# Routed steps: the key kept in a register, the opening step fed from buffered records, counters at the step's end, the result added by VectorE

## The reference

```python
def step(h, p):
    op = jnp.argmax(h[0, 0, :NOPS])
    q = h @ p['wq'][op]; k = h @ p['wk'][op]; v = h @ p['wv'][op]
    attn = softmax(einsum('bqd,bkd->bqk', q, k) * scale)
    y = einsum('bqk,bkd->bqd', attn, v) @ p['wo'][op]
    h = where(p['am'][op], y, h)
    z = relu(h @ p['w1'][op] + p['b1'][op]) @ p['w2'][op] + p['b2'][op]
    h = where(p['fm'][op], z, h)
    return h
```

## Time and profile before

| | |
|---|---|
| median of 3 runs | 333.0 us |
| profiled execution | 331.74 us |
| its span on the core | 330.0 us |
| mean granted clock of PE | 0.982 |
| busy: PE, DVE, ACT, POOL | 294.5, 189.0, 154.4, 35.1 us |
| start of the first key's `MAX8` | 246.66 us |

### The profile page before, as it was taken

How to read it: one execution, slowest core, us unless ns; L and a number is a source line. 1 busy time by engine, 2 the same in 40 slices (tenths; PEclk the granted TensorE clock), 3 DMA queues, 4 the chain that set the end, 5 groups by cost and what they waited for, 6 DMA issues and landing times.

```text
span 330.0 us, 6721 instructions
## 1 busy us (share of the span) xinstructions
PE 294.5 (89%) x2064; PEld 199.4 (60%) x2064; DVE 189.0 (57%) x452; ACT 154.4 (47%) x336; POOL 35.1 (11%) x34
## 2 busy tenths in 40 slices
PE   7999999999999989999999989989996779777980
PEld 3665677777444437898999645668952266226620
DVE  4594998883346676478887564462261156225720
ACT  2097766667154256445566033112203448644840
POOL 5300062000100014000220000024200000000010
PEclk9999999999999999999999999999998799999997
DMA  2954300000000000000000033333100100000000
GB/s 84 248 113 89 88 9 2 2 0 2 2 0 0 0 1 2 0 2 0 3 0 0 0 58 62 68 68 63 31 2 3 21 2 0 19 19 0 0 18 32
DMA packets 9386, 9.17 MB, mean 28 GB/s; under 512 B 4080, under 2 KB 8944, under 8 KB 9072
## 3 DMA queue, kind: packets, MB, share of 16 engines
q1 hardware_dynamic: 9096, 8.53, 11.7%
q10 hardware_dynamic: 264, 0.30, 0.3%
HBM read 8.57 MB, written 0.26 MB: 27 GB/s over the span
## 4 chain that ended last, share of the span: by engine, by line
PE 32%; DVE 10%; issue 4%; ACT 2%; DMA 2%; DVEq 2%; SPq 0%; POOL 0%; ACTq 0%; POOLq 0%
PE ps L759 3%; PE ps L765 3%; DMA recA<-rec_a 2%; PE ps L915 2%; PE ps L999 2%; PE ps L1055 2%; PE ps L1002 2%; PE ps L528 2%; PE ps L1047 2%; PE ps L905 1%; PE ps L897 1%; PE ps L1012 1%; PE ps L776 1%; PE ps L806 1%; DVE arena L1562 1%
## 5 line engine op out<-in xcount | busy, mean ns | idle before, releaser
L528 PE MATMUL ps<-xC,cstb 128*128 128x512 f32 (+3 forms) x134 | 57.3, 554 | 0.0
L1407 DVE TENSOR_TENSOR arena<-arena 128x512 f32 x72 | 44.3, 684 | 7.8 <-ACT arena L1107 4.6
L1114 ACT ACTIVATE arena<-ps 128x512 f32<-128x512 f32 x72 | 37.7, 603 | 15.7 <-PE ps L585 15.6
L528 PEld LDWEIGHTS ps<-xC,cstb 128*128 128x128 f32 x134 | 23.7, 192 | 24.1 <-issue 23.9
L585 PE MATMUL ps<-cstb,arena 128*128 128x128 f32 x288 | 36.3, 277 | 0.7 <-DVE arena L1407 0.7
L585 PEld LDWEIGHTS ps<-cstb,arena 128*128 128x128 f32 x288 | 31.0, 140 | 9.4 <-DVE arena L1407 8.6
L593 PE MATMUL ps<-arena 128*32 128x256 f32 x288 | 19.2, 385 | 0.0
L1275 ACT ACTIVATE arena<-ps,rmax 128x256 f32<-128x256 f32 x32 | 14.7, 479 | 2.6 <-DVE rmax L1738 2.4
L759 PE MATMUL ps<-arena 128*128 128x160 f32 x96 | 14.5, 304 | 0.3 <-DVE arena L1590 0.3
L1055 PE MATMUL ps<-arena,w2c 128*32 128x512 f32 x32 | 12.0, 719 | 1.9 <-ACT arena L1306 1.9
L497 POOL TENSOR_TENSOR arena<-w32b,cstb 128x1024 f32<-128x1024 f32 x4 | 7.6, 1893 | 57.5 <-PEq L891 45.8
(11 more groups left out here) (373 smaller groups left out, 529.0 us busy)
## 6 DMA issues: line engine op xcount, KB each, us to landing
arena<-rec_a SPq DMA_DIRECT2D x19, 128.5 KB
toepb<-toep SPq DMA_DIRECT2D x1, 1536.0 KB
w32b<-w SPq DMA_DIRECT2D x1, 1225.0 KB
cstb<-cst SPq DMA_DIRECT2D x1, 1044.0 KB
recA<-rec_a SPq DMA_DIRECT2D x4, 128.5 KB
arena<-rec_b SPq DMA_DIRECT2D x19, 16.5 KB
w1b<-moe_w SPq DMA_DIRECT2D x1, 264.0 KB
xC<-x SPq DMA_DIRECT2D x1, 256.0 KB, 2.6
```

The source lines that it names most:

```text
L528: mm(ps[bank][:, 0:cols], ident if lhs is None else lhs, (xC if rhs is None else rhs)[:, 0:cols], start=True, stop=True)
L1114: af(SQ[:, c].rearrange("p q n -> p (q n)"), ps[c % BI], ACT.Copy).then_inc(S["s_ev"], 1)
L1407: tt_(ST[:, c], hy.unsqueeze(3).to_broadcast([P, PT, 16, 16]), hx.unsqueeze(2).to_broadcast([P, PT, 16, 16]), ALU.mult).then_inc(S["prod"], 1)
```

## The change

The key's register lives through the loops: `following` loads it once at a step's end, after `op_ev`, and a turn of a loop only copies and compares it. The check of the key's bounds is gone. The counters of a step without attention are raised at its end instead of in an `Else` branch. For the opening step PE reads the key ahead of the transposes of `T` and ACT ahead of the copy of `tC`; the transposes go to PSUM bank 3, and of the three pairs of clock-keeping matmuls around them one stays. DVE copies `w2c` straight from `cacheB` and `b2c` from `recA` before the step. ACT brings in one table, with an `Exp` of 1x1, ahead of `hC`'s first copy; the 1x1 Relu is gone. The column of the table is copied to `tab_col` ahead of the attention. DVE writes `outC` from the PSUM bank in every step, just ahead of `hC`; POOL adds only where no step runs, and no longer takes part in the steps, so `op_read` counts three engines from then on. DVE waits for `op_read` ahead of `f1t`. SP stores before it waits for the last record. The 1x1 tile `f1_first` becomes `exp_first`; `tab_col` is a new tile of 1x19.

```diff
-            return eng.value_load(a, min_val=CODE0, max_val=CODE0 + NOPS * PER_OP - 1)
+            return eng.value_load(a)
...
+
+        def following(eng, key):
+
+            eng.reg_load(key, keyi[0:1, 0:1])
+            eng.reg_alu(key, key, PER_OP, ALU.mod)
...
-        def routed(eng, body, k=None):
+        def routed(eng, body, k):
+            key = eng.alloc_register("next_key")
 
             def places(levels, first):
                 with eng.Fori(0, levels[0]) as i:
-                    k = chosen(eng)
+                    k = eng.snap(key)
                     with eng.If(k >= ACTIVE):
                         n = eng.snap(first + i)
                         if len(levels) == 1:
-                            body(eng.snap(n + 1), k)
+                            body(eng.snap(n + 1), k, key)
                         else:
                             places(levels[1:], n * levels[1])
 
-            k = chosen(eng) if k is None else k
             with eng.If(k >= ACTIVE):
-                body(0, k)
+                body(0, k, key)
                 places(PLACES, 0)
...
-                sp.wait_ge(S["out_ready"], 1)
...
-                v = code_at(sp, keyi[0:1, 0:1])
+                following(sp, key)
+                v = sp.snap(key)
                 rec = record_of(sp, v)
                 sp.dma_start(recA, rec_a[bass.ds(rec, 1), :, :].to_broadcast([BI, C, REC_A])
                              ).then_inc(S["w_in"], 16)
                 sp.dma_start(recB, rec_b[bass.ds(rec, 1), :, :].rearrange("a c n -> (a c) n")
                              ).then_inc(S["wb_in"], 16)
-                with sp.If(sp.snap(v % PER_OP) < ACTIVE):
+                with sp.If(v < ACTIVE):
+                    sp.wait_ge(S["out_ready"], n + 1)
+                    settled(sp)
+                    store()
                     sp.wait_ge(S["w_in"], (n + 3) * 16)
                     settled(sp)
                     sp.wait_ge(S["wb_in"], (n + 3) * 16)
                     settled(sp)
-                    store()
...
-            def add_if_last(h_count):
-                k = chosen(pool)
-                with pool.If(k < ACTIVE):
-                    pool.wait_ge(S["h_new"], h_count)
-                    settled(pool)
-                    nc.gpsimd.tensor_tensor(outC, tC, hC, ALU.add).then_inc(S["out_ready"], 1)
-
-            def step(n, k):
-                pool.sem_inc(S["op_read"], 1)
-                pool.wait_ge(S["op_ev"], n + 2)
-                settled(pool)
-                add_if_last(n + 2)
-
             pool.wait_ge(S["ct_ev"], 4)
             pool.wait_ge(S["op_ev"], 1)
-            add_if_last(1)
-            routed(pool, step)
+            k0 = chosen(pool)
+            pool.sem_inc(S["op_read"], 1)
+            with pool.If(k0 < ACTIVE):
+                pool.wait_ge(S["h_new"], 1)
+                settled(pool)
+                nc.gpsimd.tensor_tensor(outC, tC, hC, ALU.add).then_inc(S["out_ready"], 1)
...
-            keep_busy(2)
+            pe.wait_ge(S["op_ev"], 1)
+            k0 = chosen(pe)
+            keep_busy(1)
             pe.wait_ge(S["t_sum"], 6)
-            to_C(T, 0, S["ct_mm"])
-            keep_busy(1)
-            pe.wait_ge(S["ct_ev"], 4)
-            pe.wait_ge(S["op_ev"], 1)
-
-            def step(n, k):
+            to_C(T, 3, S["ct_mm"])
+
+            def step(n, k, key):
...
+                    pe.wait_ge(S["ct_ev"], 4)
...
-                with pe.Else():
-                    pe.sem_inc(S["rq_mm"], 3)
-                    pe.sem_inc(S["rv_mm"], 1)
-                    pe.sem_inc(S["sc_mm"], B)
-                    pe.sem_inc(S["pT_mm"], B)
-                    pe.sem_inc(S["ro_mm"], BG)
-                    pe.sem_inc(S["rr_mm"], 1)
+                    pe.wait_ge(S["rt_h"], n + 1)
+                    settled(pe)
...
-                    pe.wait_ge(S["rt_h"], n + 1)
...
+                with pe.If(fl < 2):
+                    pe.sem_inc(S["rq_mm"], 3)
...
                 pe.wait_ge(S["op_ev"], n + 2)
                 settled(pe)
-
-            routed(pe, step)
+                following(pe, key)
...
+            own.link(af(exp_first, ident[0:1, 0:1], ACT.Exp))
...
-            evac_C(0, tC, 5)
-
-
+            act.wait_ge(S["op_ev"], 1)
+            k0 = chosen(act)
+            evac_C(3, tC, 5)
...
-                    own.link(af(f1_first, ident[0:1, 0:1], ACT.Relu))
-                    own.restart()
-                    act.wait_ge(S["w1_bd"], n + 1)
+                    act.wait_ge(S["w1_bd"], 2 * n + 2)
...
-            def next_op(row, place):
+            def next_op(row, col):
                 link(v_.max(top8, row))
-                link(stt(cand, row, top8[0:1, 0:1], tabf[:, :, place].rearrange("p o r -> p (o r)"),
-                         ALU.is_ge, ALU.mult))
+                link(stt(cand, row, top8[0:1, 0:1], col, ALU.is_ge, ALU.mult))
                 own.restart()
                 v_.tensor_reduce(keyi.bitcast(F32), cand, AX.X, ALU.max).then_inc(S["op_ev"], 1)
 
             dve.wait_ge(S["tab_in"], 16)
-            next_op(ln_b[0:1, 0:NOPS], slice(NB, NB + 1))
+            next_op(ln_b[0:1, 0:NOPS], tabf[:, :, NB:NB + 1].rearrange("p o r -> p (o r)"))
             dve.wait_ge(S["op_ev"], 1)
             v0 = code_at(dve, keyi[0:1, 0:1])
             first_op = slot_of(dve, v0)
             dve.wait_ge(S["cache_in"], 2 * NOPS * 16)
-            link(v_.tensor_copy(recA, cacheA.rearrange("p (o n) -> p o n", o=NOPS)[:, bass.ds(first_op, 1), :]
-                                .rearrange("p o n -> p (o n)")))
-            dve.sem_inc(S["w_in"], 16)
-            link(v_.tensor_copy(recB, cacheB.rearrange("p (o n) -> p o n", o=NOPS)[:, bass.ds(first_op, 1), :]
-                                .rearrange("p o n -> p (o n)")))
-            dve.sem_inc(S["wb_in"], 16)
-            own.restart()
-
-            def step(n, k):
+            first_a = cacheA.rearrange("p (o n) -> p o n", o=NOPS)[:, bass.ds(first_op, 1), :].rearrange(
+                "p o n -> p (o n)")
+            first_b = cacheB.rearrange("p (o n) -> p o n", o=NOPS)[:, bass.ds(first_op, 1), :].rearrange(
+                "p o n -> p (o n)")
+            v_.tensor_copy(recA, first_a).then_inc(S["w_in"], 16)
+            v_.tensor_copy(w2c, first_b).then_inc(S["w1_bd"], 1)
+            dve.wait_ge(S["w_in"], 32)
+            v_.tensor_copy(b2c, recA[:, REC_A - 1:REC_A]).then_inc(S["w1_bd"], 1)
+
+            def step(n, k, key):
+                first = isinstance(n, int)
                 fl = dve.snap(k % 4)
                 ffn = dve.snap(k % 2)
-                place = place_of(dve, k)
-                with dve.If(fl < 2):
-                    dve.sem_inc(S["w_bd"], 2)
-                    dve.sem_inc(S["rq_ev"], 1)
-                    dve.sem_inc(S["sc_max"], B)
-                    dve.sem_inc(S["sc_inv"], BG)
-                    dve.sem_inc(S["pT_evD"], B - len(TURNED_ACT))
-                    dve.sem_inc(S["rt_h"], 1)
-                dve.wait_ge(S["h_new"], n + 1)
-                dve.wait_ge(S["w_in"], (n + 2) * 16)
-                settled(dve)
+                if not first:
+                    dve.wait_ge(S["h_new"], n + 1)
+                    dve.wait_ge(S["w_in"], (n + 2) * 16)
+                    settled(dve)
...
-                v_.tensor_copy(b2c, recA[:, REC_A - 1:REC_A])
-                dve.wait_ge(S["wb_in"], (n + 2) * 16)
-                v_.tensor_copy(w2c, recB).then_inc(S["w1_bd"], 1)
-                dve.wait_ge(S["w1_bd"], n + 1)
+                if not first:
+                    v_.tensor_copy(b2c, recA[:, REC_A - 1:REC_A]).then_inc(S["w1_bd"], 1)
+                    dve.wait_ge(S["wb_in"], (n + 2) * 16)
+                    v_.tensor_copy(w2c, recB).then_inc(S["w1_bd"], 1)
+                dve.wait_ge(S["w1_bd"], 2 * n + 2)
                 dve.sem_inc(S["w_used"], 1)
+                place = place_of(dve, k)
+                link(v_.tensor_copy(tab_col, tabf[:, :, bass.ds(place, 1)].rearrange("p o r -> p (o r)")))
+                own.restart()
...
+                dve.wait_ge(S["op_read"], 3 * n + 4)
+                settled(dve)
...
-                dve.wait_ge(S["op_read"], 4 * n + 4)
                 settled(dve)
-                next_op(ps[0][0:1, 0:NOPS], bass.ds(place, 1))
...
+                next_op(ps[0][0:1, 0:NOPS], tab_col)
+                with dve.If(fl < 2):
+                    dve.sem_inc(S["w_bd"], 2)
...
+                dve.wait_ge(S["op_ev"], n + 2)
+                settled(dve)
+                following(dve, key)
+                dve.wait_ge(S["ct_ev"], 4)
                 with dve.If(ffn != 0):
                     dve.wait_ge(S["f2mm"], n + 1)
+                    stt(outC, ps[1], b2c, tC, ALU.add, ALU.add).then_inc(S["out_ready"], 1)
                     ts_(hC, ps[1], b2c, None, ALU.add).then_inc(S["h_new"], 1)
                 with dve.Else():
+                    tt_(outC, tC, hC, ALU.add).then_inc(S["out_ready"], 1)
```

(2 more changed lines are left out.)

41 lines of the change are left out of this document (26 added, 15 removed).

## The result

| | kernel before | changed kernel |
|---|---|---|
| median of the runs, us | 333.1 (332.04 to 333.67) | 324.11 (322.56 to 325.98) |
| ratio, 95% interval | | 0.9755 (0.9722 to 0.9787) |
| profiled execution, us | 331.74 | 325.98 |
| its span, us | 330.0 | 324.2 |

The kernel is about 2.5% (9 us) faster; the kernel before was run twice more than the three times given above. The forecast was 323.4, so the measured median is 0.7 above it and inside the range.

The account below looks back on a forecast made before the run. Bounds: issue time before the opening FFN, DVE's loop-head key reads, record fetches, and SP's walk at the end. 4.4 + 1.2 + 0.6 + 1.9 - 1.1 - 0.95 + 3.5 = 9.55 us off 331.74, plus 1.26 to the median: 323.4, range 320.8 to 327.2.

Parts of the forecast that it names:

- Opening step: First MAX8 to the opening record's DMA: PE's early key read brings the DMA to 253.7 from 258.09, 4.4 us won.
- Key chain: From key to record DMA in steps 1 to 3: 0.4 us a step won on DVE, 0.2 on SP.
- Entry into step 1: DVE's first multiply of step 1 comes 0.45 us behind the record instead of 2.35: 1.9 us won.
- What is added: Costs the change puts on the chain: 1.1 us for PE's wait, 0.95 for the tab_col copy, nothing for outC.
- (a): PE's wait for rt_h ahead of register and branch instructions costs 0.55 us in each of two attention steps, 1.1.
- (b): The tab_col copy and op_read test on DVE cost 0.75 us in step 2, 0.1 each in steps 1 and 3.
- (c): outC ahead of hC makes the state 0.75 us later each step, hidden by the wait for the record: cost nothing.
- The end: SP's store and walk through the loops: walk of 6.8 us becomes 3.75, store's issue moves away, 3.5 us won.
- A: Rival: PE's clock still falls in the opening step, costing 1.0 us, 324.4; chance 0.13.
- B: Rival: the end does not shorten as counted and wins 1.5 us instead of 3.5, 325.4; chance 0.12.
- C: Rival: the added PE wait and tab_col copy cost double, 4.1 us instead of 2.05, 325.5; chance 0.09.
- D: Rival: the clock falls in an attention step behind PE idle of 2.8 us or more, up to 14.6 us, 338; chance 0.02.

Follow-up runs that it names:

- pe_open: The changed kernel with PE's opening step in the order of before (transposes of T first, key read after tC's copy): 325.85 us, ratio 0.9786.
- pool_early: The changed kernel with POOL reading the first key ahead of its wait for tC: 323.26 us, ratio 0.9711.
- no_check: The kernel before with only the key's bounds check left out where the key is read: 329.55 us, ratio 0.9899.
- reload: The changed kernel with the key read from SBUF again at each loop head, without a bounds check: 326.43 us, ratio 0.9825.
- rt_back: The changed kernel with PE's wait for rt_h back at the FFN's first matmul: 323.7 us, ratio 0.9712.
- col_early: The changed kernel with the copy into tab_col at the step's start, ahead of the wait for the record: 322.64 us, ratio 0.9703.
- store_late: The changed kernel with SP's store behind the wait for the last record, as before: 324.49 us, ratio 0.9759.
- again: The changed kernel itself, unedited, run and profiled once more as base for the other runs: 323.58 us, ratio 0.9759.
- no_fetch: The changed kernel with SP testing the key first, so no record is fetched or waited for behind the last step: 323.87 us, ratio 0.9755.

## Why the prediction was right

**Opening step**: right. The DMA goes at 254.14, 6.74 behind the first MAX8 against 11.43: 4.7 won, 4.4 forecast. The order of what is last was as put: `tC`, POOL's load (0.51), DVE's test, `f1t`. The first FFN matmul starts at 250.57, 0.6 later than forecast, and this cost nothing since POOL was later still. `pe_open` and `pool_early` show it: PE's hidden layer is only 0.2 us from being last itself.

**Key chain**: right on DVE, wrong on SP. From PE's last matmul to the end of the key the chain is 0.43 us shorter a step (forecast 0.4). SP was to win 0.2 a step; from the key to the DMA the changed kernel needs 0.77, 0.93, 0.93 and 0.90 us against 0.97, 0.94, 0.94 and 0.94: 0.2 in the opening step and 0.01 to 0.04 behind it. The check did go, as `no_check` shows with its 0.66 to 0.69. What the step missed is that the load got longer. The loads of the key of SP in the changed kernel, and below them those of `reload` (ns min/median/max):

```profile
L309 SPq TENSOR_LOAD <-keyi x4: 285/444/453, 253.5 to 314.8; - x4
```

```profile
L309 SPq TENSOR_LOAD <-keyi x4: 264/269/280, 252.9 to 313.7; - x4
```

In `reload`, as before, another load of the key in the loop heads comes between the record's DMA and this one, and there this one takes 0.27 and the loop head's first one up to 0.45. In every kernel here the first load that SP makes behind its two record DMAs took 0.43 to 0.46. Keeping the key in a register took the cheap loads away and left the dear one, moved onto the path from key to DMA. That is 0.17 us a step, and the one term of the prediction's sum whose mechanism failed.

**Entry into step 1**: right in kind. DVE multiplies 0.45 behind the record, as said. The stretch won 1.59, not 1.9, as the DMA of before had taken 4.15 us and not the 4.0 that I carried over from the next fetch, and the one of the changed kernel 4.32.

**What is added**: (a) 0.46 us in step 1 and 0.61 in step 3 (0.72 and 0.75 where there were 0.26 and 0.14), forecast 0.55; confirmed by `rt_back`, which takes 0.58 back. (b) 0.87 us in step 2, forecast 0.75; nothing measurable in steps 1 and 3. Confirmed by `col_early`, which also shows that 0.6 of it could be avoided. (c) hidden, as said.

**The end**: 3.14 of 3.5 won. The walk took 3.8 (forecast 3.75), and `store_late` agrees with the store's 0.45. The term itself was 0.2 too large by its own rows: four turns of 0.55 (328.6 to 329.15) are 2.2 us and not 2.4. With loads of 0.6 us the forecast would have been 322.2 on the median (323.4 less 1.2), not 320.9. What is missing lies ahead of the walk: it started 4.33 us behind the last record's issue (315.61 to 319.94), where the store of before went out 3.95 behind it (318.46 to 322.41).

**Rivals.** A (clock falls in the opening step) did not come: the opening FFN ran at 1.00 in every profile with the change, even in `pe_open`. B and C did not come. D was right that a clock could fall in an attention step, and wrong in size: in the changed kernel the fall came in step 3, behind an idle of 1.75 us and not 2.8, and it cost 1.55 us, not 14.6. In `reload` it came in step 1, as D had it, behind an idle of 1.65, and cost 1.5 to 1.7. I had priced it as if the clock stayed down through the whole attention, but the window shows 0.53 for some 3.6 us and 1.00 behind. The cover was said to be the same as that of before; it was, but what it has to cover grew with `tab_col`'s place and the longer DMA: PE's idle ahead of step 3 was 1.00 us before. The sum held nothing for it.

**How near the number is.** The sum gave 322.2 us for a profiled execution, and the one of "again", which had no fall of the clock, took 323.82. Of these 1.6 us, 0.9 are what the stretches won less than forecast (8.66 against 9.55: the end 0.36, step 2's fetch 0.44, the entry into step 1 0.31, less 0.3 that the opening won more), and 0.7 is the later first `MAX8`, which the prediction took from an early execution. The 1.26 us that it added to get from that execution to the median covered a part of both, so that the forecast lies 0.2 to 0.7 below the two medians (323.58 and 324.11) is in part luck. A fall of the clock in an attention adds 1.5 to 1.7 us in the executions that have one.

What stays open: what decides in a given execution. PE's idle ahead of step 3 was 1.75, 1.50, 1.75, 1.65 and 1.31 us where the clock fell in the attention behind it, and 1.45, 1.39, 0.99, 0.93, 0.56, 0.32 and 2.23 in the profiles of kernels with the change where it did not; `pe_open` stood idle for 1.61 in the opening step and kept its clock. Falls also came in other places: near 211, in the FFN of step 2 (`pool_early`), in the last FFN (`no_fetch`, `store_late`). Why the same record's DMA takes 3.6 to 4.5 us is open too. No run took these apart.

## What to carry to other kernels

When a register value is taken out of loops, ask which of the loads that vanish was the slow one, since in this kernel the next load of that queue became as slow. Of two engines that are nearly level at a gate, freeing one is worth only the distance to the other, so free both or neither. Where PE's idle grows to more than it was before, look at its clock in the stretch behind it over several executions: a pair of filler matmuls may buy a steadier time even where it buys no median. And lay profiles of two kernels against each other from the first event that the edit can touch: the part ahead of it differed by 0.6 to 0.7 us here between executions of the same code.

## What the runs showed of the hardware that was not expected

- A load of one word from SBUF into SP's register took 0.26 to 0.29 us, but 0.43 to 0.46 as the first one behind two DMA issues, in all kernels of this case. Right behind the store's issue it took 0.72 or 0.73 (before and `no_check`), and 0.45 where it came 2.3 us behind it (`reload`).
- A fall of TensorE's clock in an attention cost 1.5 to 1.7 us here (22.37 to 22.55 against 20.90 for the stretch of step 3): the matmuls of `L979` and `L990` took 1.47 and 2.06 us instead of 0.89 and 1.11, and those behind them had their old durations.
- In the attention of step 3 (and of step 1 in `reload`) the falls appeared behind idles of 1.3 to 1.75 us, and in the same program an idle of 1.75 us had one (the changed kernel) and one of 1.45 had none ("again"); behind the idle of 2.9 us in the opening step of before the clock was low in both profiles that had it (before and `no_check`).
- On SP, one turn of a loop nest with no load in it still cost 0.65 to 0.86 us in register and branch instructions.
- One DVE instruction over 128x2 near the start of the program took 0.17 us in eight profiles and 1.02 to 1.26 in six, with the same code (0.17 in before, 1.22 in `no_check`). What holds it no run shows.
